# Layer one of a gated Flamingo stack: the second pair's rows prepared inside the first pair's scores, and maxima on four PSUM banks

## The chip, the cores and the metric

One core of one Trainium2 chip runs the whole program. TensorE (PE) multiplies matrices and transposes into PSUM, which has eight banks of 128 x 512 words. VectorE (DVE) and ScalarE (ACT) read PSUM; GpSimd (POOL) works on SBUF; SyncE (SP) issues transfers. The metric is the device time of one execution in microseconds (us).

## The reference

Four batches of 256 tokens x 256 features pass four layers, each with a gated attention and a gated feed-forward part. The change lies in the attention of layer one. Its setup fixes 16 heads of 16, keys and values from a 64-wide context:

```python
return {'q': jax.random.normal(k1, (B, S, H), dtype=jnp.float32), 'latent_kv': jax.random.normal(k2, (B, S, L), dtype=jnp.float32), 'Wq': ..., 'Wkv_expand': ..., 'Wout': ...}
```

What the kernel computes for each batch: rows of x are normalised (mean, variance); queries are their product with Wq; keys and values are the product of the context with Wkv; per head there is a causal softmax of the scores over 256 x 256; the weighted values of all heads go through Wout, and the result, times a gate, is added to x. Then comes the feed-forward part of layer one (ternary weights, 8-bit rows, a Hadamard transform), and layers two and three.

## The kernel before

**Tiling.** A token row lies on a partition; a batch is two tiles of 128 tokens (T = 2). Layer one's attention works on pairs of batches: turn i = 0 takes batches 0 and 1, turn i = 1 takes 2 and 3; inside a turn s = 0 or 1 is the batch. Every engine has its own instruction stream, in an order written out by hand, and waits on semaphores.

**Banks.** `plan(stage, i, ...)` gives each PSUM fill (a key such as `("max", 0, 3)`) a bank, in turn over a group's list of banks. A fill waits until its bank's previous fill has been read (`empty`); a reader waits until the fill is counted (`full`). In layer one, group A has the banks [4, 5], B the double banks [0, 2] (0-1 and 2-3), V the double bank 6-7.

**A turn's work, in PE's order.**
- `queries1`, `key_values1`: projections of a batch into B. ACT (`query_parts1`, `key_parts1`, L2149, L2156) writes their bf16 leading parts; DVE (`query_parts1`, `key_parts1`, L2817, L2827) writes the rests, the three-part split that lets bf16 products stand for float32. For s = 1 POOL finishes the parts (`parts1`, L949).
- `qsT`, `ksT` (`turn_column1`): the parts turned, four fills each for s = 0; ACT moves the queries out, DVE (`turned_keys`, L2805) the keys. For s = 1 they are the four double fills `cols`, between the maxima, moved by ACT.
- `max1` / `maximum1`: scores once more, only for their row maxima: 12 fills of a batch, which DVE reduces (L2851). The maxima are split and turned (`shift_rows1`, `shT`, L2864) and put by a small transfer into two rows of the queries' stack; PE waits for it (`shift_in`).
- `exp1` (L1405, L1407): the scores of two heads with the maximum taken off, 16 for a turn (g = 0 to 15); ACT exponentiates (L2182). `values1` (L1421) multiplies by the values, once for two `exp1`.
- `tokens1` turns the sums back to rows, DVE divides (`weighted1`, L2873, L2875), `turn_heads` turns them again, ACT moves them, `project` (L1446) multiplies by Wout, DVE adds into x (`add_projected`, L2882).
- `norm_next` (L2437 to L2471) normalises the next pair's rows; `turn_next` turns them, `queries1` follows.

**Other work on DVE.** `advance(largest, n)` does n pieces of the top-k search of layer two's adjacency, alternately two MAX8 (L2679) and two MATCH_REPLACE8 pairs (L2684); a 20th piece of a batch is L2687 and L2691. These pieces are spread by hand into places where DVE would wait.

**Between the two turns.** After the last `values1` and `project(0, 0)`, PE turns batch 2 and 3's rows, then interleaves batch 1's heads with the second pair's projections. `project(0, 1)` goes into bank 5 of A; `qsT` of turn 1 begins at bank 4, its second fill at bank 5.

Of the kernel before, what the change touches and what calls it, by code (L numbers as in the profile page):

```python
# [7 lines left out]
BF16 = mybir.dt.bfloat16  # L8
# [163 lines left out]
def flamingo_gated(nc, x, ctx_512, g_xattn, g_ffn, W_k0, b_k0, ln_gamma, ln_beta, gate_w, gate_b, expert_w, expert_b,  # L172
                   Wq1, Wkv1, Wout1, w_gate, w_up, w_down, Wq2, Wk2, gamma_raw, w12, w3, router_w, expert_bias,
                   sw1, sw2, sw3, W_router, W_sgate, Ws_gate_up, Ws_down, We_gate_up, We_down, consts, out):
    with ExitStack() as ctx:
# [316 lines left out]
        def plan(stage, i, **groups):  # L492
# [4 lines left out]
            for g, (firsts, wide, keys) in groups.items():  # L497
                f = pl.setdefault(stage, {}).setdefault(g, None) or Fills(sem(f"filled_{stage}{g}"))
# [29 lines left out]
        def max_order1():  # L528

            first = [("qsT", 0, k) for k in range(4)] + [("ksT", 0, k) for k in range(4)]  # L530
            for k in range(12):
                first += [("cols", 1, k // 3)] * (k % 3 == 0) + [("max", 0, k)]
            first += [("max", 1, 0), ("max", 1, 1), ("shT", 0)]
            return first + [("max", 1, k) for k in range(2, AHEAD1)]
# [5 lines left out]
        for i in range(TURNS):  # L540
            plan("l1x", i,
                 A=([4, 5], 1, [key for key in max_order1() if key[0] != "cols"]
                    + [("max", 1, k) for m in rest_at1 for k in rest_at1[m]] + [("shT", 1)]
                    + [("tok", 0, 0), ("tok", 0, 1), ("oT", 0), ("out", 0)]
                    + ([("xT", 0), ("xT", 1)] if i < TURNS - 1 else [("AT", 0), ("AT", 1)])
                    + [("tok", 1, 0), ("tok", 1, 1), ("oT", 1), ("out", 1)]),
                 B=([0, 2], 2, [("q", 0), ("kv", 0), ("q", 1), ("kv", 1)] + [("cols", 1, k) for k in range(4)]
                    + [("sc", s, k) for s in range(2) for k in range(NH1 // 2)]),
                 V=([6], 2, streams([("pv",)])))
        plan("prep1b", 0, A=([0, 1, 2, 3], 1, [("tern", w, k) for w in range(2) for k in range(2)]))  # L550
# [184 lines left out]
        def _(sp):  # L735
# [58 lines left out]
            f = pl["l1x"]["A"]  # L794
            for i in range(TURNS):
                for s in range(2):
                    sp.wait_ge(f.drained(i, ("shT", s)), f.read(i, ("shT", s)))
# [354 lines left out]
        def _(pe):  # L1152
# [207 lines left out]
            fa, fb = pl["l1x"]["A"], pl["l1x"]["B"]  # L1360
# [6 lines left out]
            def turn_column1(i, name, s, k):  # L1367
# [6 lines left out]
                else:  # L1374
                    turn(fa, i, (name, s, k), column_blocks(stack[s], pitch, 4 * k, 0), identb, BF16)

            def shift1(i, s):
                pe.wait_ge(shift_ready["l1x"].sem, shift_ready["l1x"].count(2 * i + s))
                turn(fa, i, ("shT", s), [(2 * NH1, t * P, sh1[s][:, t * 2 * NH1:(t + 1) * 2 * NH1]) for t in range(T)],
                     identb, BF16)  # L1380

            def max1(i, s, k):

                if k == 0:
                    for f, key in ([(fa, ("qsT", 0, 2)), (fa, ("qsT", 0, 3)), (fa, ("ksT", 0, 2)), (fa, ("ksT", 0, 3))] if s == 0
                                   else [(fb, ("cols", 1, 2)), (fb, ("cols", 1, 3))]):
                        pe.wait_ge(f.drained(i, key), f.read(i, key))
                pe.wait_ge(fa.drained(i, ("max", s, k)), fa.empty(i, ("max", s, k)))
                v = fa.slot(i, ("max", s, k))
# [6 lines left out]
                mm.then_inc(fa.filled, 1)  # L1396
# [13 lines left out]
            def values1(i, s, k):  # L1410

                fv = pl["l1x"]["V"]
                if k == 0:
                    pe.wait_ge(fv.drained(i, ("pv", s)), fv.empty(i, ("pv", s)))
                for m in (2 * k, 2 * k + 1):
# [23 lines left out]
            def project(i, s):  # L1439

                pe.wait_ge(fa.drained(i, ("oT", s)), fa.read(i, ("oT", s)))
                pe.wait_ge(fa.drained(i, ("out", s)), fa.empty(i, ("out", s)))
                v = fa.slot(i, ("out", s))
# [4 lines left out]
                mm.then_inc(fa.filled, 1)  # L1448
# [18 lines left out]
            def queries_turned1(i):  # L1467
                for k in range(4):
                    turn_column1(i, "qsT", 0, k)

            def scores1(i):

                for name, s, *k in max_order1():
                    if name == "max":
                        max1(i, s, *k)
                    elif name == "shT":
                        shift1(i, s)
                    elif name != "qsT":
                        turn_column1(i, name, s, *k)
                for g in range(NH1):  # L1480
# [12 lines left out]
                    if g == 12:  # L1493
                        tokens1(i, 0)
                    elif g == 14:
                        turn_heads(i, 0)
                values1(i, 1, 3)
                project(i, 0)
# [9 lines left out]
            turn_next("l1x", 0)  # L1508
            next_turned(fa, 0)
            queries1(1, 0)  # L1510
            tokens1(0, 1)
            key_values1(1, 0)
            turn_heads(0, 1)
            queries1(1, 1)
# [2083 lines left out]
```

## Time and profile before

| | |
|---|---|
| median of 3 runs | 772.85 us (770.63 to 774.46) |
| the profiled execution, its own time | 765.34 us |
| its span | 763.5 us |
| mean granted TensorE clock | 0.966 |
| PE busy | 670.3 us, 88% |
| DVE busy | 539.0 us, 71% |
| ACT busy | 351.9 us, 46% |
| POOL busy | 215.9 us, 28% |

Times in the rows count from the start of the span. Layer one's attention runs from 113 to 246 us. A timeline row gives start, length, engine, line, operation, tiles, count and, in brackets, how long its engine sat idle before it and what ended that. A PE row with a count has matmuls that overlap, so its length is that of the group.

### The profile page before, as it was taken

The numbers are of one execution on the slowest core, as the hardware profiler recorded it, in microseconds if no ns is written. First come the engines' busy times: TensorE is split into PE (matmuls) and PEld (weight loads), VectorE is DVE, ScalarE is ACT, GpSimd is POOL, SyncE is SP. The second block draws the span as 40 slices with busy tenths as digits, with TensorE's granted clock in tenths as the row PEclk, the third lists the DMA queues.
The fourth block names the chain that finished last, engine by engine and source line by source line (L and its number), as shares of the span: only waits on it lengthen the run. The fifth ranks groups of instructions, "written<-read, shape, count | busy, mean of one in ns | idle before, by whom it ended". The sixth has DMA issues, their size and how long they took to land. (4 is left out here: it accounts for less than half of the span.)

```text
span 763.5 us, 13913 instructions
## 1 busy us (share of the span) xinstructions
PE 670.3 (88%) x4446; PEld 457.7 (60%) x4446; DVE 539.0 (71%) x1622; ACT 351.9 (46%) x620; POOL 215.9 (28%) x308
## 2 busy tenths in 40 slices
PE   9999987897889877798889999976788999999997
PEld 4644565665666556567666787653243327777776
DVE  5787988879686597888887454546987967525545
ACT  2673445565454765432204524326478895212220
POOL 1002596001100023301333553643334220533330
PEclk9999999999899999999999999998789999999999
DMA  7996421040000050000034151012000034133314
GB/s 181 341 249 135 157 86 56 2 168 1 2 3 2 1 166 1 1 1 1 29 114 171 57 178 59 29 50 77 1 2 3 2 119 111 63 105 105 98 56 172
DMA packets 55565, 60.23 MB, mean 79 GB/s; under 512 B 13847, under 2 KB 48808, under 8 KB 55496
## 3 DMA queue, kind: packets, MB, share of 16 engines
q1 hardware_dynamic: 50408, 46.02, 21.2%
q0 software_dynamic: 4848, 13.28, 5.0%
q8 instruction: 38, 0.62, 0.4%
q14 instruction: 31, 0.25, 0.1%
q10 hardware_dynamic: 240, 0.05, 0.0%
HBM read 34.92 MB, written 24.20 MB: 77 GB/s over the span
## 5 line engine op out<-in xcount | busy, mean ns | idle before, releaser
L2016 ACT ACTIVATE arenas<-psum 128x512 f32<-128x512 f32 (+6 forms) x89 | 63.2, 732 | 58.5 <-PE psum L1175 50.6
L3295 DVE TENSOR_REDUCE arenas<-psum 128x2 f32<-128x512 f32 x96 | 61.8, 684 | 12.0 <-PE psum L1767 10.7
L1175 PE MATMUL psum<-conb,shared 128*128 128x128 bf16 (+2 forms) x512 | 41.1, 239 | 12.1 <-issue 8.1
L983 POOL TENSOR_SCALAR arenas<-arenas,small 128x1024 f32<-128x1024 f32 x8 | 9.0, 1124 | 150.9 <-DVE small L2986 150.9
L1175 PEld LDWEIGHTS psum<-conb,shared 128*128 128x128 bf16 (+2 forms) x512 | 36.0, 125 | 20.3 <-issue 17.8
L1000 POOL DMA_INDIRECT experts_l<-shared,small x30 | 29.7, 989 | 63.1 <-ACT shared L2318 52.7
L2016 ACT ACTIVATE late<-psum 128x512 f32<-128x512 f32 (+1 forms) x51 | 25.6, 502 | 42.6 <-PE psum L1175 42.5
L1175 PE MATMUL psum<-con,early 128*128 128x128 f32 (+1 forms) x188 | 32.2, 281 | 12.9 <-ACT late L2016 5.1
L2365 ACT ACTIVATE early<-psum 128x1024 f32<-128x1024 f32 x32 | 32.0, 1031 | 17.3 <-PE psum L1784 17.0
L1651 PE MATMUL psum<-arenas,early 128*128 128x256 f32 x160 | 36.7, 383 | 0.7 <-DVE arenas L3449 0.7
L2182 ACT ACTIVATE late<-psum 128x768 f32<-128x768 f32 x32 | 25.3, 811 | 24.7 <-PE psum L1407 24.5
L2851 DVE TENSOR_REDUCE arenas<-psum 128x2 f32<-128x512 f32 (+1 forms) x48 | 31.4, 686 | 6.9 <-PE psum L1394 6.5
L1651 PE MATMUL psum<-early,late 128*128 128x256 f32 x128 | 30.9, 388 | 5.9 <-DVE early L3188 5.8
L1175 PEld LDWEIGHTS psum<-con,early 128*128 128x128 f32 (+1 forms) x188 | 21.5, 143 | 23.6 <-ACT late L2016 8.1
L1148 POOL DMA_INDIRECT experts_l<-late,shared x23 | 22.0, 958 | 48.0 <-DVE shared L3469 41.9
L2365 ACT ACTIVATE late<-psum 128x1024 f32<-128x1024 f32 x32 | 31.4, 1062 | 5.0 <-PE psum L1784 5.0
L1175 PE MATMUL psum<-con,arenas 128*128 128x128 f32 x194 | 29.3, 279 | 4.9 <-DVE arenas L2471 2.6
L1164 PE MATMUL psum<-conb 128*128 128x512 bf16 x128 | 31.9, 401 | 1.8 <-POOLq L891 1.8
L2016 ACT ACTIVATE shared<-psum 128x256 f32<-128x256 f32 (+2 forms) x38 | 16.3, 429 | 36.8 <-PE psum L1175 31.6
L1651 PEld LDWEIGHTS psum<-arenas,early 128*128 128x128 f32 x160 | 29.8, 190 | 5.6 <-DVE arenas L3449 1.1
L3260 DVE TENSOR_TENSOR shared<-shared,psum 128x128 f32<-128x128 f32 x30 | 8.6, 287 | 33.7 <-PE psum L1720 19.6
L1720 PE MATMUL psum<-late,shared 128*128 x120 | 32.1, 390 | 0.2 <-issue 0.2
(455 smaller groups left out, 1770.4 us busy)
## 6 DMA issues: line engine op xcount, KB each, us to landing
sorted_l<-late SPq DMA_DIRECT2D x3, 1920.0 KB, 16.7
early<-sorted_l SPq DMA_DIRECT2D x6, 645.0 KB, 5.8
early<-in_L_ffn_sw SPq DMA_DIRECT2D x3, 1024.0 KB, 9.3
late<-sorted_l SPq DMA_DIRECT2D x23, 129.0 KB, 2.1
sorted_l<-late SPq DMA_DIRECT2D x1, 2944.0 KB, 23.2
early<-in_L_ffn_We_gate_up SPq DMA_DIRECT2D x2, 1408.0 KB
early<-in_L_ffn_expert_w SPq DMA_DIRECT2D x2, 1024.0 KB, 6.8
early<-in_L_ffn_w SPq DMA_DIRECT2D x1, 2048.0 KB, 8.4
```

Of the source, the lines that this page charges most:

```text
L983: pool.tensor_scalar(ha[s][:, rows], ha[s][:, rows], c2[s][:, t:t + 1], ROUND, ALU.mult, ALU.add)
L1000: pool.indirect_dma_start(expert_rows2[p], bass.IndirectOffsetOnAxis(dest2[p][:, i:i + 1], 0), out_r2[k], None).then_inc(outs_sent[k], 16)
L1148: pool.indirect_dma_start(expert_rows, bass.IndirectOffsetOnAxis(dest[i], 0), out_r[i % OUTS], None).then_inc(out_sent[i % OUTS], 16)
L1164: pe.matmul(v, onesb, onesb.unsqueeze(1).broadcast_to([P, BANK // P, P]), start=True, stop=True)
L1175: last = pe.transpose(v[0:parts, at:at + k], src, idn[0:k, 0:k])
L1651: mm = pe.matmul(v[0:rows, half * S:(half + 1) * S], w[:, c * width + at:c * width + at + rows], xT[s][:, c * S:(c + 1) * S], start=(c == ...
L1720: mm = pe.matmul(fu.slot(p, ("up", i))[:, 0:2 * H_R2], xT_r2[i % 2][:, c * P:(c + 1) * P], w12T[:, bass.ds(which[i] * (2 * H_R2) + c * E * ...
L2016: act.activation(dst, view(v), ACT.Copy, scale=scale).then_inc(f.drained(i, key), 1)
L2182: act.activation(q3d(pexp1[m % 4], 2, S + P), q3d(v, 2, BANK)[:, :, 0:S + P], ACT.Exp, scale=HD1 ** -0.5).then_inc(fb.drained(i, ("sc", s, ...
L2365: act.activation(pexp3[w // 4][m % 4], f.slot(0, ("sc", w, m)), ACT.Exp, scale=HD3 ** -0.5)\
L2851: dve.tensor_reduce(dst, q3d(v, heads, BANK // heads), X, ALU.max, negate=True) .then_inc(fa.drained(i, ("max", s, k)), 1)
L3295: dve.tensor_reduce(nm, q3d(f.slot(0, ("max", w, k)), 2, S), X, ALU.max, negate=True)\
```

## The change

1. Group A's early fills (`qsT`, `ksT`, the maxima of s = 0 and the first six of s = 1, `shT` of s = 0) become a group M over four banks [6, 7, 4, 5]; V still uses 6-7, and its first `values1` waits until the maxima there are read. `max1`'s waits for turned columns are made finer.
2. In turn 0, `turn_next("l1x", 0)` (the second pair's rows turned) stands at g = 14 of the scores; `next_turned` and `queries1(1, 0)` come ahead of the last `values1`. ACT moves the turned rows between the last two exponentials and takes `query_parts1(1, 0)` before `sums1(0, 1)` and `moved_heads(0, 0)`.
3. Batch 0's `turn_heads` moves behind the last `values1`. `project(0, 0)` comes after the second pair's `key_values1`, `queries1` and two of the four `qsT`; the other two `qsT` come behind `turn_heads(0, 1)`.
4. `project(0, 1)` and its `add_projected` move into turn 1, behind `shT` of batch 2, on a bank of M.
5. DVE: `weighted1(0, 0)` comes right after `norm_next`; `query_parts1(1, 0)` and the others are put between; 34 pieces of `advance` stay 34 but are dealt out anew (15 in turn 0 and 19 in turn 1, where there were 16 and 18).

```diff
             for g, (firsts, wide, keys) in groups.items():
-                f = pl.setdefault(stage, {}).setdefault(g, None) or Fills(sem(f"filled_{stage}{g}"))
+                f = pl.setdefault(stage, {}).setdefault(g, None)
+                f = f or Fills(None if (stage, g) == ("l1x", "V") else sem(f"filled_{stage}{g}"))
...
+        def out_at1(i, s):
+            return (1, ("out", 1, 0)) if (i, s) == (0, 1) else (i, ("out", s))
...
-            first += [("max", 1, 0), ("max", 1, 1), ("shT", 0)]
+            first += [("max", 1, 0), ("max", 1, 1), ("shT", 0)] + [("out", 1, 0)] * i
             return first + [("max", 1, k) for k in range(2, AHEAD1)]
...
             plan("l1x", i,
-                 A=([4, 5], 1, [key for key in max_order1() if key[0] != "cols"]
-                    + [("max", 1, k) for m in rest_at1 for k in rest_at1[m]] + [("shT", 1)]
-                    + [("tok", 0, 0), ("tok", 0, 1), ("oT", 0), ("out", 0)]
-                    + ([("xT", 0), ("xT", 1)] if i < TURNS - 1 else [("AT", 0), ("AT", 1)])
-                    + [("tok", 1, 0), ("tok", 1, 1), ("oT", 1), ("out", 1)]),
+                 M=([6, 7, 4, 5], 1, [key for key in max_order1(i) if key[0] != "cols"]),
+                 A=([4, 5], 1, [("max", 1, k) for m in rest_at1 for k in rest_at1[m]] + [("shT", 1)]
+                    + [("tok", 0, 0), ("tok", 0, 1)]
+                    + ([("xT", 0), ("xT", 1), ("oT", 0), ("tok", 1, 0), ("tok", 1, 1), ("out", 0), ("oT", 1)] if i == 0
+                       else [("oT", 0), ("out", 0), ("AT", 0), ("AT", 1),
+                             ("tok", 1, 0), ("tok", 1, 1), ("oT", 1), ("out", 1)])),
...
                 if k == 0:
                     pe.wait_ge(fv.drained(i, ("pv", s)), fv.empty(i, ("pv", s)))
+                    for n in range(AHEAD1 - 4, AHEAD1):
+                        pe.wait_ge(fm.drained(i, ("max", 1, n)), fm.read(i, ("max", 1, n)))
...
                     if g == 12:
                         tokens1(i, 0)
+                    elif g == 14 and i == 0:
+                        turn_next("l1x", 0)
                     elif g == 14:
                         turn_heads(i, 0)
+                if i == 0:
+                    next_turned(fa, 0)
+                    queries1(1, 0)
                 values1(i, 1, 3)
+                if i == 0:
+                    turn_heads(0, 0)
+                    key_values1(1, 0)
+                    tokens1(0, 1)
+                    queries1(1, 1)
+                    queries_turned1(1, range(2))
                 project(i, 0)
...
             scores1(0)
-            turn_next("l1x", 0)
-            next_turned(fa, 0)
-            queries1(1, 0)
-            tokens1(0, 1)
-            key_values1(1, 0)
             turn_heads(0, 1)
-            queries1(1, 1)
-            project(0, 1)
-            queries_turned1(1)
+            queries_turned1(1, range(2, 4))
             key_values1(1, 1)
             scores1(1)
...
+                    if g == 14 and i == 0:
+                        move_next(fa, 0)
+                if i == 0:
+                    query_parts1(1, 0)
+                    sums1(0, 1)
+                    moved_heads(0, 0)
+                else:
+                    moved_heads(i, 0)
+                    sums1(i, 1)
...
             def scores1(i):
-                advance(largest, (3, 4)[i])
+                advance(largest, 3)
                 turned_keys("l1x", i, 0, 4, K1 + 2, kT1)
...
                 if i == 0:
+                    advance(largest, 2)
                     for n in range(2, B):
                         experts_added0(n)
                     dve.drain()
                 norm_next("l1x", i)
-                advance(largest, (2, 5)[i])
-                weighted1(i, 0)
-                advance(largest, 4)
-                add_projected(i, 0)
-                if i == 1:
+                if i == 0:
+                    weighted1(0, 0)
+                    advance(largest, 5)
+                    query_parts1(1, 0)
+                    weighted1(0, 1)
+                    key_parts1(1, 0)
+                    query_parts1(1, 1)
+                    advance(largest, 2)
+                    add_projected(0, 0)
+                else:
+                    advance(largest, 5)
+                    weighted1(1, 0)
+                    advance(largest, 5)
+                    add_projected(i, 0)
                     symmetric(fa, i, 1)
-                advance(largest, (4, 2)[i])
-                weighted1(i, 1)
+                    advance(largest, 3)
+                    weighted1(i, 1)
+                    advance(largest, 3)
```

## Rows read from the trace of the kernel before

**Rows 1.** Busy time of each engine by stretch of layer one's attention; PEclk is the granted clock.
```profile
132.80:147.50 14.70, 11.46 (x156) 9.41 (x154) 12.07 (x23) 7.50 (x4) 2.32 (x3) 1.00 0.02 4
147.50:171.00 23.50, 21.63 (x302) 16.57 (x301) 18.83 (x58) 14.96 (x19) 0.00 (x0) 1.00 0.40 136
171.00:198.00 27.00, 21.91 (x134) 15.94 (x133) 20.08 (x53) 11.71 (x15) 2.32 (x3) 0.81 0.00 1
```

**Rows 2.** DVE's timeline, turn 0: keys moved, then the maxima.
```profile
128.59 1.29 DVE L2805 COPY arenas<-psum 98x1024 bf16<-98x1024 bf16 x2
132.23 0.69 DVE L2840 TENSOR_TENSOR late<-psum,shared 128x512 f32<-128x512 f32 x1 [0.20 <-issue]
...
133.50 2.10 DVE L2851 TENSOR_REDUCE arenas<-psum 128x4 f32<-128x512 f32 x3
...
141.33 1.99 DVE L2851 TENSOR_REDUCE arenas<-psum 128x2 f32<-128x512 f32 x3 [0.54 <-PE psum L1394]
...
144.97 0.27 DVE L2864 COPY arenas<-psum 32x256 bf16<-32x256 bf16 x1
```

**Rows 3.** PE's timeline: the first score of each turn.
```profile
147.80 0.28 PE L1405 MATMUL psum<-arenas 98*128 98x256 bf16 x1 [0.16 <-DMA arenas<-arenas]
...
213.45 0.28 PE L1405 MATMUL psum<-arenas 98*128 98x256 bf16 x1
```

**Rows 4.** PE's timeline between the turns.
```profile
166.78 0.66 PE L1175 MATMUL psum<-con,late 128*128 128x128 f32 x4
...
176.84 1.98 PE L1463 MATMUL psum<-early,arenas 64*128 64x512 f32 x4
...
180.98 1.93 PE L1446 MATMUL psum<-early,late 128*128 128x256 f32 x8
182.75 0.61 PE L1175 MATMUL psum<-conb,shared 128*96 128x128 bf16 x8
186.73 1.29 PE L1175 MATMUL psum<-conb,shared 128*96 128x128 bf16 x16 [3.37 <-issue]
```

**Rows 5.** DVE's timeline between the turns.
```profile
158.12 1.41 DVE L2437 BATCH_NORM_STATS2 small<-xs 128x6 f32<-128x256 f32 x4
...
163.53 0.75 DVE L2679 MAX8 small<-early 128x8 f32<-128x256 f32 x2
...
165.30 0.26 DVE L2873 RECIPROCAL arenas<-psum 128x16 f32<-128x16 f32 x1
...
166.64 0.74 DVE L2679 MAX8 small<-early 128x8 f32<-128x256 f32 x2
...
173.31 0.43 DVE L2687 TENSOR_SCALAR early<-early 128x512 f32<-128x512 f32 x1
...
174.90 0.76 DVE L2679 MAX8 small<-adj 128x8 f32<-128x256 f32 x2 [0.20 <-issue]
...
178.02 0.68 DVE L2791 TENSOR_TENSOR late<-psum,shared 128x512 f32<-128x512 f32 x1
...
182.18 0.69 DVE L2791 TENSOR_TENSOR late<-psum,shared 128x512 f32<-128x512 f32 x1 [0.24 <-issue]
...
185.88 0.75 DVE L2882 SCALAR_TENSOR_TENSOR xs<-psum,small,xs 128x512 f32<-128x512 f32 x1
```

**Rows 6.** DVE's timeline before turn 1's scores.
```profile
199.24 2.11 DVE L2851 TENSOR_REDUCE arenas<-psum 128x4 f32<-128x512 f32 x3
```

**Rows 7.** Busy time by stretches of 1 us, with the granted clock.
```profile
109.00:110.00 1.00, 0.00 (x0) 0.00 (x0) 0.92 (x3) 0.36 (x1) 1.00 (x2) 1.00 0.39 131
...
187.00:188.00 1.00, 1.00 (x15) 0.80 (x12) 1.00 (x5) 0.61 (x1) 0.71 (x2) 0.71 0.00 0
...
197.00:198.00 1.00, 1.00 (x15) 1.00 (x14) 0.72 (x2) 0.00 (x0) 0.00 (x0) 0.67 0.00 0
```

**Rows 8.** ACT's timeline between the turns.
```profile
169.91 1.01 ACT L2167 COPY arenas<-psum 128x1024 f32<-128x1024 f32 x1 [0.57 <-PE psum L1421]
...
176.08 1.51 ACT L2136 ACTIVATE shared<-psum 128x1024 bf16<-128x1024 f32 x2 [2.10 <-PE psum L1455]
```

## What I expect, and from what

> **What bounds the kernel now.** First the page's table of shares: PE is busy 88% of the span and DVE 71%, so a change in the order of work is worth what PE's idle time in its stretch is worth, and what TensorE loses to a low clock there. Then busy time by stretch [rows 1]: in the first turn's maxima (132.8 to 147.5) PE works 11.5 of 14.7 us and DVE 12.1; in the scores that follow PE works 21.6 of 23.5, PE sets the pace and nothing is to be had; between the turns (171 to 198) PE works 21.9 of 27.0 at a mean granted clock of 0.81. So two places hold slack: the maxima (twice) and the stretch between the turns. Then each engine's timeline. In the maxima DVE reduces three fills at a rhythm of 0.65 us and then idles 0.54 [rows 2], since two banks let PE be only two fills ahead and the turned `cols` come in between: a ping-pong. Between the turns PE stands still for 3.37 us until 186.73 [rows 4]. The trace names no releaser; it is the second `qsT`, on bank 5, which `add_projected(0, 1)` has to read first, and that DVE does at 185.88 to 186.63 [rows 5], behind everything else in its queue. Just after it the clock is at half (granted 0.50, which is 1.2 of 2.4 GHz), 187.3 to about 197.6 [rows 7].
>
> **Turn 0's maxima on four banks.** Keys: DVE starts moving them at 128.59 and today waits for the last two; with four banks all four are turned by then, so 4 x 0.65 = 2.6 us, to 131.2; then 0.1, and 1.27 for the values' part (132.23 to 133.50) gives the first maximum at 132.55 instead of 133.50, 0.95 less [rows 2]. The 12 maxima of s = 0 now take 133.50 to 143.32 = 9.8 us; without the waits 12 x 0.65 = 7.8, so 2.0 less. PE can hold that: three fills with their `cols` cost 0.89 + 3 x 0.34 = 1.9 us against DVE's 1.95 (my estimate from PE's rhythm; between the first and last maxima PE is busy 78% in rows 1), so they are nearly even, and if PE starts late it does not catch up. I take 2.5 of 2.95; the bounds are 1.5 (PE's late start costs one group) and 3.0. The transfer of the shift, 145.24 to 147.80 [rows 2, 3], stays. The first score then stands at 145.3 instead of 147.8. The prologue's queries on four banks gain nothing: the following `key_values1` waits for bank 2, which DVE frees at 124.5 either way.
>
> **Scores of turn 0.** 22 us to the last `values1`, PE's own work, unchanged. `turn_next` at g = 14 takes the place of `turn_heads` (166.78 [rows 4], so 164.1 now). It waits for the normalised rows. DVE, 2.5 earlier: two more pieces ahead (1.77, the pair from 163.53 to 165.30), two expert additions, then the normalising, 158.12 to 163.53 [rows 5]; shifted by 1.8 - 2.5 it ends at 162.85, 1.2 us in time. `weighted1(0, 0)` right behind (1.34, 165.30 to 166.64) frees bank 4 at 164.2, when PE wants it at 164.5: hidden, with little to spare.
>
> **Between the turns, walked through on PE** (durations: 8 transposes 0.9, a `queries1` or `project` 1.8, a `key_values1` 1.9, from the starts in rows 4; a pair of ACT's parts 1.5, the copy of the sums 1.0 [rows 8]). Rows turned to 165.0; last `exp1` and `values1` to 166.35; ACT's two moves are done by 166.1, so `next_turned` doesn't hold; `queries1(1, 0)` to 168.1; last `values1` 168.9; `turn_heads(0, 0)` 169.4; `key_values1(1, 0)` 171.3; `tokens1(0, 1)` wants ACT's copy (parts 168.2 to 169.7, copy to 170.7): ready; to 172.2; `queries1(1, 1)` to 174.0; two `qsT` (DVE's parts done at 172.0) to 174.9; `project(0, 0)` to 176.6; `turn_heads(0, 1)` to 177.1. All gaps of this stretch are filled up to here. The third `qsT` stands on bank 4, last filled by `("out", 0)`. So the wait is not removed; it changes its name to `add_projected(0, 0)`.
>
> When does DVE get there? It idles from 168.2 until ACT's parts at 169.7. Query parts 2.2 (178.02 to 182.18, less two pieces 1.8 and a gap) to 172.0; `weighted1(0, 1)` to 173.3; key parts 2.9 (182.18 to 185.88, less one piece 0.8), behind ACT, to 176.4; rest of the second queries 0.7 to 177.1; two pieces, one of them the long last one, 2.4 (173.31 to 175.66) to 179.5; `add_projected` 0.7 to 180.2 [rows 5]. PE stands 3.1 us, 177.1 to 180.2, almost what it stood before. Queued behind it: the two `qsT`, `key_values1(1, 1)`, `ksT` and all maxima. After it two `qsT` 0.9, `key_values1` 1.9, `ksT` 1.8: 184.9; DVE follows the keys, 183.6 to 186.2, and after 1.5 us for the values the maxima of turn 1 start at 187.7. Before it was 199.24 [rows 6]. From the first score of turn 0 this is 187.7 - 145.3 = 42.4 us against 199.24 - 147.80 = 51.4 [rows 3, 6]: 9.0 less, full clock assumed. It holds `project(0, 1)` (1.8) moved away, the idle bits ahead of 186.73 filled with work, and about 4.9 of work at half clock (from 186.73 to 198.12 PE does some 6.5 us of full-clock work).
>
> **Turn 1.** Four banks again: 2.0 less. `project(0, 1)`, 1.8 us on PE, falls into the wait for the shift's transfer, which is 2.5 us, so it costs nothing there; without that cover, 1.8. On DVE its addition (0.75) comes before the maxima 2 to 5 of s = 1, so the fills at g = 0 to 3 find banks 4 and 5 late, and PE loses some 0.7. The first score moves from 213.45 [rows 3] to 200.0 at full clock. At the end `weighted1(1, 1)` comes behind three pieces (2.6) instead of two (2.4 by the same rows): 0.3 with the rounding. The last three pieces fall under `turn_heads` and `project(1, 1)`. 15 + 19 pieces are 34, as before, so nothing goes to later stages.
>
> **Sum at full clock.** 2.5 + 9.0 + 2.0 - 0.7 - 0.3 = 12.5 us less.
>
> **The clock.** 3.37 us of idle PE before 186.73 were followed by half clock [rows 4, 7]. 1.85 us of idle, nearly all of 109 to 110.8, were not [rows 7]. The new wait of 3.1 us is nearer to the first. Right behind it stand 5.5 us of work that the maxima wait for. Bounds: nothing (no fall), and 4.7 (all of it and the first fills at half, as before). I take 2.5, about half. That is the forecast: 12.5 - 2.5 = 10.0 less. The Trainium skill, page "TensorE: Matmul & The Clock Gate", section "What's actually happening", says that the low clock is the default state and that activity releases it, and that there are just two levels. Rows 7 agree on the levels (a second of 0.71 or 0.67 is one that holds the step). By that rule the change is suspect in one more place, the next paragraph's second rival: whoever lets PE finish its maxima early buys it idle time.
>
> Against the profiled execution's 765.34 us this gives 755.3; the runs' median is 772.85, 7.5 above the profiled one, and the same 10.0 off it gives 762.9 us, 1.3% less. The measurement of this kernel tells some 0.5%, 3.9 us, from no change.
>
> **Rivals.**
> - *No fall of the clock in the new wait* (3.1 instead of 3.4 us of idle). For: 1.85 us did nothing. Against: the nearness of the two numbers. 12.5 less: 760.4. Chance 0.22.
> - *The clock falls already in turn 0.* With four banks PE waits 1.4 us for the shift's rows, works about 1.9 and then waits 1.9 for the transfer, where before the longest such wait was 0.5; then come the scores, PE's own work. Some 5 us at half cost 2.5, and with the full 4.7 later the gain is about 5.5: 767.3. For: the two idle pieces add up to 3.3. Against: there is work between them, and DVE-bound stretches ran at 1.00 in rows 1. Chance 0.15.
> - *The gain is given back.* The feed-forward part starts 10 us earlier and runs into something that was not waited for, or the deferred work costs as much as it saves (stalls at bank 4 for the rows' turning, at banks 4 and 5 in turn 1, 1.8 of uncovered projection). Then 0 to 4 less, 769 to 773. Against: the loads of the next weights are out by 171 and DVE's pieces are the same 34. Chance 0.12.
> - *Slower.* The same fall at the first score of turn 0 that lasts: PE's 21.6 us of scores [rows 1] at half clock take up to 21.6 more, a net 9 slower, 782. The point: low-clock work beyond 25 us in total (half of it is lost) eats 12.5. The longest low stretch here is 10 us [rows 7]. Chance 0.03.
> - The forecast itself: 0.48.
>
> **Numbers.** 762.9 us. The range of 8 in 10 leaves out the slow case and most of the given-back one on one side and a full-clock run with a lucky reading on the other: 758.0 (12.5 less, and 2.4 for the spread of the runs, which is 3.8 wide) to 769.0 (the second rival with the same allowance). Faster by over 0.5%: forecast, first and second rival, and a third of the given-back case: 0.88. Within: 0.09. Slower: 0.03.
>
> **What would show it.** First score of turn 0 at 145 to 146.3, DVE's maxima in one row of 0.65 without 0.5 gaps. An idle PE of about 3 us behind `turn_heads(0, 1)` that ends with `add_projected` (L2882's counterpart), with half clock behind it or not: this is the term I am least sure of. `turn_next` without a wait at g = 14. Maxima of turn 1 from 188 to 191. First score of turn 1 at 200 to 203, `project(0, 1)` just ahead of it with little idle time. I am wrong if DVE reaches `add_projected(0, 0)` much later, if the rows at g = 14 aren't ready, if clock falls multiply, or if the stages behind layer one's attention don't move up with it.

## The result, and the profile after

The changed kernel took 760.8 us (median of 4 runs, 758.5 to 761.6) against 773.1 (770.6 to 774.5): a ratio of 0.9863, with a 95% interval of 0.9823 to 0.9903. Forecast were 762.9 us in a range of 758.0 to 769.0.

The page of the changed kernel, its head and the busy time of the engines:

```profile
span 756.7 us, 13927 instructions
PE 666.9 (88%) x4446; PEld 457.0 (60%) x4446; DVE 538.1 (71%) x1622; ACT 351.2 (46%) x620; POOL 216.6 (29%) x308
```

The same work, 6.8 us less span than the trace of before. The two traces are one execution each, so the change is read from a stretch that both have: from the first key that DVE moves in turn 0 to the first reduction of the feed-forward part. Called the stage below, it took 118.25 us (128.59 [rows 2] to 246.84) and now takes 108.57 (130.24 to 238.81): 9.7 less. The rest of the difference is not the change's: the stage starts 1.65 later, behind a low-clock stretch at 111 to 119 that the trace of before did not have, and what follows it is 1.2 longer. The medians of the timed runs differ by 12.3 us, the ratio makes it 10.6, and 9.7 lies inside its interval (7.5 to 13.7 us).

The trace of before has a low clock of its own inside the stage, while the keys are turned, behind a wait of PE of 1.80 us. PE's row there, then DVE's, then 1 us of the clock:

```profile
129.39 3.59 PE L1175 MATMUL psum<-conb,shared 128*98 128x128 bf16 x32 [1.80 <-issue]
```

```profile
130.48 0.69 DVE L2805 COPY arenas<-psum 98x1024 bf16<-98x1024 bf16 x1 [0.60 <-PE psum L1175]
131.34 0.69 DVE L2805 COPY arenas<-psum 98x1024 bf16<-98x1024 bf16 x1 [0.16 <-PE psum L1175]
```

```profile
130.00:131.00 1.00, 1.00 (x13) 1.00 (x12) 0.52 (x1) 0.00 (x0) 0.00 (x0) 0.50 0.00 0
```

The last two keys come 0.86 us apart, the pace of turned keys at half clock in the changed kernel's turn 1 too (187.37, 188.22, 189.08). At full clock PE turns one in about 0.5 us (four in 1.99 us at 128.14 in the changed kernel), so the third would have been ready some 0.4 earlier and the fourth would not have held DVE. By this estimate about 0.5 us of what the keys give back below is the clock of that one execution and not the banks.

DVE's timeline of the changed kernel, turn 0, against [rows 2]:

```profile
130.24 2.49 DVE L2835 COPY arenas<-psum 98x1024 bf16<-98x1024 bf16 x4
...
134.21 7.46 DVE L2882 TENSOR_REDUCE arenas<-psum 128x4 f32<-128x512 f32 x12
...
143.32 0.27 DVE L2896 COPY arenas<-psum 32x256 bf16<-32x256 bf16 x1
```

All four keys in one row, and all 12 maxima without a gap: 7.5 us where 9.8 stood. The shift is copied 9.1 us after the first maximum begins, not 11.5. PE has become the engine that waits here, as its timeline shows (rows of the shift, then the first score, against [rows 3]):

```profile
142.35 0.27 PE L1188 MATMUL psum<-conb,arenas 128*32 128x128 bf16 x2 [1.00 <-DVE arenas L2890]
146.15 0.28 PE L1421 MATMUL psum<-arenas 98*128 98x256 bf16 x1 [1.81 <-DMA arenas<-arenas]
```

PE between the turns, against [rows 4]: the rows turned at g = 14 (no wait), then everything without a gap up to 178.4, then the wait.

```profile
164.86 1.07 PE L1188 MATMUL psum<-con,arenas 128*128 128x128 f32 x8
...
175.98 1.95 PE L1464 MATMUL psum<-early,late 128*128 128x256 f32 x8
177.77 0.60 PE L1188 MATMUL psum<-con,late 128*128 128x128 f32 x4
181.91 1.06 PE L1188 MATMUL psum<-conb,shared 128*96 128x128 bf16 x16 [3.54 <-issue]
182.90 3.41 PE L1481 MATMUL psum<-early,arenas 64*128 64x512 f32 x4
```

The trace names no releaser; DVE's timeline does, by time:

```profile
177.51 0.68 DVE L2855 TENSOR_TENSOR late<-psum,shared 128x512 f32<-128x512 f32 x1
178.11 0.42 DVE L2717 TENSOR_SCALAR early<-early 128x512 f32<-128x512 f32 x1
178.62 1.41 DVE L2721 SCALAR_TENSOR_TENSOR early<-adj,small,early 128x256 f32<-128x256 f32 x2
180.23 0.75 DVE L2709 MAX8 small<-adj 128x8 f32<-128x256 f32 x2 [0.20 <-issue]
181.06 0.75 DVE L2914 SCALAR_TENSOR_TENSOR xs<-psum,small,xs 128x512 f32<-128x512 f32 x1
...
192.09 7.47 DVE L2882 TENSOR_REDUCE arenas<-psum 128x4 f32<-128x512 f32 x12
```

L2914, `add_projected(0, 0)`, ends at 181.8 and PE goes on at 181.9. The clock behind it, by stretches of 1 us:

```profile
182.00:183.00 1.00, 1.00 (x17) 0.92 (x16) 0.93 (x4) 0.44 (x1) 0.00 (x0) 1.00 0.00 0
183.00:184.00 1.00, 1.00 (x2) 0.53 (x3) 0.93 (x6) 1.00 (x2) 0.00 (x0) 0.66 0.00 0
184.00:185.00 1.00, 1.00 (x2) 0.33 (x1) 0.38 (x1) 0.49 (x1) 0.00 (x0) 0.50 0.00 0
...
190.00:191.00 1.00, 1.00 (x19) 1.00 (x18) 0.80 (x2) 0.00 (x0) 0.00 (x0) 0.93 0.00 0
```

Turn 1 of the changed kernel on PE: the projection moved there, and the first score.

```profile
200.45 1.99 PE L1464 MATMUL psum<-early,late 128*128 128x256 f32 x8
...
204.70 0.28 PE L1421 MATMUL psum<-arenas 98*128 98x256 bf16 x1 [0.64 <-DMA arenas<-arenas]
```

Of the 1.8 us that PE waited for the same transfer in turn 0, 0.6 are left here: the projection stands inside it.

### The profile page after: what moved, and what is told of

It is laid out like the page before. It is cut to its first block and busy times, and to the rows that moved or that the text cites. A ratio compares the mean times of both kernels' runs of the same rounds, so it can differ in the third digit from the quotient of the medians.

```text
span 756.7 us, 13927 instructions
## 1 busy us (share of the span) xinstructions
PE 666.9 (88%) x4446; PEld 457.0 (60%) x4446; DVE 538.1 (71%) x1622; ACT 351.2 (46%) x620; POOL 216.6 (29%) x308
## 5 line engine op out<-in xcount | busy, mean ns | idle before, releaser
L3338 DVE TENSOR_REDUCE arenas<-psum 128x2 f32<-128x512 f32 x96 | 61.8, 684 | 12.1 <-PE psum L1791 10.7
L1188 PE MATMUL psum<-conb,shared 128*128 128x128 bf16 (+2 forms) x512 | 38.0, 230 | 9.6 <-issue 4.5
L1188 PEld LDWEIGHTS psum<-conb,shared 128*128 128x128 bf16 (+2 forms) x512 | 33.5, 118 | 17.3 <-issue 14.8
L1161 POOL DMA_INDIRECT experts_l<-late,shared x23 | 22.1, 962 | 48.6 <-DVE shared L3512 42.5
L1177 PE MATMUL psum<-conb 128*128 128x512 bf16 x128 | 31.6, 398 | 1.8 <-POOLq L904 1.8
```

The costliest lines, as they stand in the source:

```text
L1177: pe.matmul(v, onesb, onesb.unsqueeze(1).broadcast_to([P, BANK // P, P]), start=True, stop=True)
L1188: last = pe.transpose(v[0:parts, at:at + k], src, idn[0:k, 0:k])
L3338: dve.tensor_reduce(nm, q3d(f.slot(0, ("max", w, k)), 2, S), X, ALU.max, negate=True)\
```

## The experiments

Twelve runs of eleven kernels. All stage times are from one trace each; "between" is from the first score of turn 0 to the first maximum of turn 1. "Wait" is PE's wait ahead of the turned fills or, where named, elsewhere; "low clock" is where, between the turns or in turn 1's maxima, the granted clock is under 1, to the whole us. The ratio is to the kernel before on the same chip.

| kernel | keys to first score | between | turn 1 to its first score | to the end | stage | wait, low clock between the turns | ratio (95% interval) |
|---|---|---|---|---|---|---|---|
| before | 19.21 | 51.44 | 14.21 | 33.39 | 118.25 | 3.37, 187-198 | 1 |
| changed | 15.91 | 45.94 | 12.61 | 34.11 | 108.57 | 3.54, 183-191 | 0.9863 (0.9823-0.9903) |
| changed, again | 15.92 | 46.93 | 13.18 | 34.39 | 110.42 | 3.53, 180-191 | 0.9875 (0.9814-0.9935) |
| changed, third time | 15.90 | 46.10 | 12.81 | 34.30 | 109.11 | 3.54, 184-192 | 0.9889 (0.9854-0.9924) |
| four banks alone | 15.91 | 49.31 | 12.47 | 33.83 | 111.52 | 2.92, 188-195 | 0.9892 (0.9862-0.9923) |
| maxima on two banks | 18.34 | 46.32 | 16.37 | 34.09 | 115.12 | 3.54, 183-191 | 0.9963 (0.9925-1.0002) |
| heads weighed late | 15.91 | 51.25 | 13.05 | 34.32 | 114.53 | 4.02 and 3.54, 166-171 and 187-195 | one run |
| wait filled | 16.23 | 44.58 | 12.43 | 33.87 | 107.11 | 0.5, none | one run |
| add first | 15.90 | 42.81 | 14.01 | 34.25 | 106.97 | 0.6, none; 1.48, 187-191 later | 0.9807 (0.9737-0.9877) |
| keys and values first | 15.90 | 42.51 | 12.63 | 34.14 | 105.18 | 1.62, 182-187 | 0.9793 (0.9727-0.9859) |
| both | 15.90 | 42.81 | 13.75 | 34.36 | 106.82 | 0.28, none; 1.49, 191-195 later | 0.9801 (0.9741-0.9861) |
| rows late | 15.91 | 49.18 | 12.70 | 34.28 | 112.07 | 4.08, 184-195 | 0.9924 (0.9898-0.9949) |
| projection back | 15.92 | 48.77 | 11.89 | 35.68 | 112.26 | 3.58, 183-187 | one run |
| DVE's pieces dealt anew | 17.01 | 40.94 | 12.45 | 34.09 | 104.49 | 0.28, none | 0.9792 (0.9752-0.9832) |

**The changed kernel again**, unedited:

> The changed kernel once more, on the chip that also runs the three below. Times of the stage are taken in the trace from the first key that DVE moves in turn 0 to the first reduction of the feed-forward part: 118.25 us in the kernel before, 108.57 in the changed one. Theory (the walk along the engines' queues): 108.6 again, give or take 1.7 or 3.4 us where the clock falls once more or once less, and 1.2 to 1.7% less than before in time. Rival (the gain of the timed runs, 12.3 us, is more than the stage's 9.7 because of low-clock stretches elsewhere that have nothing to do with the change): the stage is as said, but the time moves by several us either way from one call to the next.

Stage 110.4, with the low clock 11 us long behind the same wait of 3.53 us, and ratio 0.9875: the gain repeats, and the stage moves by 1.9 us, with low clock at 180 to 191 as what differs. The third trace of the same kernel, at the end of the table, has 109.1 and 0.9889, where 108.6 or 110.3 and 0.980 to 0.988 had been expected. Against before, whose low clock between the turns was also 11 us long, the second trace is 7.8 shorter and not 9.7.

**Four banks alone.** The kernel before with group M, its waits, and nothing reordered:

```diff
-                 A=([4, 5], 1, [key for key in max_order1() if key[0] != "cols"]
-                    + [("max", 1, k) for m in rest_at1 for k in rest_at1[m]] + [("shT", 1)]
+                 M=([6, 7, 4, 5], 1, [key for key in max_order1() if key[0] != "cols"]),
+                 A=([4, 5], 1, [("max", 1, k) for m in rest_at1 for k in rest_at1[m]] + [("shT", 1)]
```

> The kernel before with the four banks alone: group M with its fills on banks 6, 7, 4, 5 and the waits that belong to it, all orders of PE, ACT and DVE as before. Theory: keys 0.9 less, maxima 2.4 less in each turn, the stall between the turns stays (the third turned fill stands on bank 4 behind add_projected(0, 1)) but two fills come ahead of it, 0.5 less: stage 118.25 - 6.2 = 112.0, time about 6 us less than before (ratio 0.992). Rival (the banks do it all, since the first two turned fills of turn 1 no longer wait for add_projected): the stage comes to 109 and the time to the changed kernel's.

Stage 111.5, forecast 112.0: 6.7 of the 9.7 us. Some 1.7 of these 6.7 is that the low clock between the turns lasted 7 us here and 11 before. The first theory holds; the wait between the turns is there, 2.9 us, two fills later than before. In time, 0.9892 cannot be told from the changed kernel's 0.9863 to 0.9889; the traces can, 111.5 against 108.6, with a low clock of nearly the same length behind the wait (against the changed kernel's other two traces it is 1.1 and 2.4).

**Maxima on two banks**, all else as in the changed kernel:

```diff
-                 M=([6, 7, 4, 5], 1, [key for key in max_order1(i) if key[0] != "cols"]),
+                 M=([6, 7, 4, 5] * 2 + [4, 5] * 10, 1, [key for key in max_order1(i) if key[0] != "cols"]),
```

> The changed kernel with only the maxima (and the shift and the projection among them) put back on banks 4 and 5; the turned queries and keys keep four. Theory: 2.4 more in turn 0 and 1.6 to 2.4 in turn 1, stage 112.6 to 113.4, time 4 to 5 us above the changed kernel. Rival (DVE was not held by the banks but by the order of the turned columns): stage 109 to 110, DVE's gaps between the reductions as long as with four banks.

Turn 0 gives back 2.4 us, as said, DVE's gaps of 0.5 are there again. Turn 1 gives back 3.8, more than said, so the stage is 115.1 where 112.6 to 113.4 was forecast, and the time 7.2 us above the changed kernel's on this chip where 4 to 5 was. DVE's timeline there shows why:

```profile
204.86 0.27 DVE L2896 COPY arenas<-psum 32x256 bf16<-32x256 bf16 x1
207.10 0.75 DVE L2914 SCALAR_TENSOR_TENSOR xs<-psum,small,xs 128x512 f32<-128x512 f32 x1 [1.97 <-PE psum L1464]
207.77 2.80 DVE L2882 TENSOR_REDUCE arenas<-psum 128x4 f32<-128x512 f32 x4
```

The projection waits for a bank, the maxima behind it for `add_projected`, and so the first score comes 4.8 us after the shift's copy and not 3.5. Moving the projection there is nearly free only because the banks are four: the two parts of the change lean on each other.

**Heads weighed late:**

```diff
-                    weighted1(0, 0)
                     advance(largest, 5)
+                    weighted1(0, 0)
```

> The changed kernel with one line moved: DVE does its five search pieces (4.4 us) before it weighs batch 0's heads and no longer after. Theory: the turned rows at g = 14 need banks 5 and 4, which that weighing frees, so PE stands some 4.0 us in the middle of the last scores and all that follows is 4.0 later: stage 112.6, and 1.7 to 3.4 more if the clock falls behind such a wait. Rival (the order of heads and search pieces is hidden, since DVE idles 1.4 us ahead of the queries' parts anyway): stage at most 1 us longer.

PE's timeline, the turned rows at g = 14:

```profile
167.22 1.94 PE L1188 MATMUL psum<-con,arenas 128*128 128x128 f32 x8 [4.02 <-DVE late L2907]
```

4.02 us for 4.0 forecast, and a low clock that begins within the wait, at 166, and lasts to 171. With both, "between" is 5.3 longer and the stage 114.5, in the 114.3 to 116.0 that the theory gave with a fall. The heads' weighing is where the reordering could have gone wrong; its margin is below half a microsecond (in the changed kernel it frees bank 5 at 164.5, and PE wants it at 164.9).

**Wait filled.** PE multiplies constants into an empty bank while it waits (`kept_busy` issues these products):

```diff
             turn_heads(0, 1)
+            kept_busy(fb, 1, ("kv", 1), 14)
             queries_turned1(1, range(2, 4))
```

> The changed kernel with 14 idle products of 512 columns on the still empty bank of the second pair's last keys and values, placed where PE waits for add_projected(0, 0). They compute nothing that is used. Their length is 3.0 us, as the wait. Theory (the wait costs twice: its own 3.5 us, and the half clock behind it): the third turned fill still starts when DVE has added, but the granted clock stays at 1.00, so the maxima of turn 1 start 2.9 us earlier after the first score (45.9 less 2.9, so 43.0) and the stage is 105.7. Rival (the low clock comes from elsewhere, or costs nothing as DVE sets the pace there): 45 to 46 and a stage of 108 to 109.

PE after the filled wait:

```profile
178.71 3.19 PE L1177 MATMUL psum<-conb 128*128 128x512 bf16 x14
182.41 1.06 PE L1188 MATMUL psum<-conb,shared 128*96 128x128 bf16 x16 [0.52 <-issue]
183.41 1.98 PE L1481 MATMUL psum<-early,arenas 64*128 64x512 f32 x4
185.32 2.88 PE L1188 MATMUL psum<-conb,shared 128*98 128x128 bf16 x48
```

The granted clock was 1.00 in each of 180 to 191. The same work takes 1.98 and 2.88 us where it took 3.41 and 4.72. From its start to the first maximum of turn 1 are 7.55 us (182.41 to 189.96), against 10.18 (181.91 to 192.09): 2.6 us for the low clock alone, with the wait kept. "Between" is only 1.4 shorter, since this execution had a low stretch at 146 to 150, at the first scores of turn 0, which is the second rival of the prediction, and its turned fills start 37.0 us after the first score and not 35.8. That is most of the reason why the stage came to 107.1 and not to the 105.7 of the theory.

**Three edits that take the wait away**, the first two together in the third:

```diff
                     query_parts1(1, 1)
-                    advance(largest, 2)
                     add_projected(0, 0)
+                    advance(largest, 2)
```

> The changed kernel with DVE's add_projected(0, 0) ahead of two search pieces (2.4 us) and not behind them. Theory: it runs at the end of project(0, 0), the stall of 3.5 us shrinks to some 0.6, the clock does not fall, and then DVE's five pieces hold the keys: maxima of turn 1 4.1 us earlier (41.8 after the first score), stage 104.5, time 0.5% under the changed kernel's. Rival (DVE is the bound there, the stall is only the other side of it): maxima at most 1 us earlier.

```diff
             turn_heads(0, 1)
+            key_values1(1, 1)
             queries_turned1(1, range(2, 4))
-            key_values1(1, 1)
             scores1(1)
```

> The changed kernel with key_values1(1, 1), 1.9 us of PE's work that has to wait for nothing, ahead of the two turned fills and so inside the stall. Theory: 1.7 us of the stall are left, no fall of the clock behind it, and DVE's pieces hold the keys: maxima of turn 1 3.7 us earlier (42.3), stage 104.9. Rival (what is left of the wait still drops the clock): 44 and 106.5.

> Both of the last two edits. Theory: PE no longer waits, DVE's queue alone sets the start of turn 1's maxima, so it adds nothing to either: 41.8 to 42.0 after the first score, stage 104.5. Rival (both stalls were PE's and add up): 39.9 and 102.5.

Maxima of turn 1 at 42.8, 42.5 and 42.8 us after the first score, where 41.8, 42.3 and 41.8 to 42.0 were forecast: 3.1 to 3.4 earlier than in the changed kernel, and together no more than alone. So beyond the wait it is DVE's queue that holds: in all three it goes from its search pieces to the keys without idling. One part of a theory failed: with keys and values first, the 1.62 us that is left of the wait still had a low clock behind it, 182 to 187; since DVE's pieces hold the keys, it cost next to nothing ahead of the maxima, 42.5 for 42.3. With DVE adding first, something new appears; PE in that kernel:

```profile
177.20 1.06 PE L1188 MATMUL psum<-conb,shared 128*96 128x128 bf16 x16 [0.59 <-issue]
178.19 1.98 PE L1481 MATMUL psum<-early,arenas 64*128 64x512 f32 x4
180.10 2.88 PE L1188 MATMUL psum<-conb,shared 128*98 128x128 bf16 x48
187.39 1.85 PE L1188 MATMUL psum<-conb,shared 128*96 128x128 bf16 x16 [1.48 <-issue]
```

PE is early, makes the first maxima, and then waits for DVE's values part to free a bank for the second `cols`; the clock falls at 187, and from the first maximum of turn 1 to the copy of the shift are then 10.7 us and not 9.1. The kernel with both edits does the same (1.49 us, low at 191 to 195). That eats half of the gain: stages of 107.0 and 106.8, where 104.5 was forecast for both; the kernel that uses the wait for keys and values has 105.2, forecast 104.9. The three ratios (0.979 to 0.981) cannot be told from one another, and this chip's runs of before were slower (785.3 us), so they are not set against ratios from another chip.

**Rows late**, the second pair's rows turned behind the last `values1`:

```diff
-                    elif g == 14 and i == 0:
-                        turn_next("l1x", 0)
...
                 values1(i, 1, 3)
                 if i == 0:
+                    turn_next("l1x", 0)
+                    next_turned(fa, 0)
+                    queries1(1, 0)
                     turn_heads(0, 0)
```

> The changed kernel with the second pair's rows turned after the last values1 and not at g = 14, and ACT's two moves after the last exponential. Theory: PE does the same work but then waits 0.5 to 0.7 us for ACT's moves, and the queries' parts reach DVE 1.5 us later; DVE's chain up to add_projected moves by that, PE's stall stays at 3.5, so all is 1.5 us later: 47.4 us from the first score to the maxima of turn 1, stage 110.1 (low clock as in the changed kernel). Rival (the place of the turning is what the change lives on, all of the order's 5 us): 51 and 113.5.

49.2 and 112.1, 1.8 and 2.0 above the forecast and 1.8 and 1.4 below the rival's, so the totals do not choose. The parts do: the turned fills start 37.8 us after the first score and not 35.8, which is 2.0 and not the 1.5 forecast (the queries' parts reach DVE 2.1 later, and PE's wait is 4.1); the other 1.2 comes behind the wait, with a low clock of 11 us and not 8. The place of the turning is worth some 2.0 us and what the clock adds.

**Projection back** between the turns (its addition behind the first one on DVE and its bank in group A are not shown):

```diff
             turn_heads(0, 1)
+            project(0, 1)
             queries_turned1(1, range(2, 4))
```

> The changed kernel with project(0, 1) back between the turns, behind turn_heads(0, 1), and its addition right behind the first one on DVE. Theory: 1.8 us of projection and 0.7 of addition come on the path between the turns, 2.6 in all, and 0.7 comes back in turn 1, where the project and its addition are gone from ahead of the maxima: 48.5 from the first score to the maxima of turn 1, stage 110.5. Rival (the projection fits into the stall as before, so its move gains nothing): 46 and 108.

48.8 between, forecast 48.5: 2.8 more than in the changed kernel, against 2.6 (its low clock between the turns was 4 us shorter, and it had one of 4 us at the first scores of turn 0, which about cancel). Turn 1 gets to its first score 0.7 sooner, and there PE waits 1.74 us for the transfer, where the projection had stood; a low clock at 206 to 211 follows, in PE's own scores, and the stretch to the end is 1.6 longer; so the stage is 112.3 where 110.5 was forecast. The projection's place gives 2.8 us between the turns, takes 0.7 of it back in turn 1, and may save a fall of the clock.

**DVE's pieces dealt anew**, with the two edits of before (34 pieces still):

```diff
                     weighted1(0, 0)
-                    advance(largest, 5)
+                    advance(largest, 6)
...
-                    advance(largest, 2)
                     add_projected(0, 0)
+                    advance(largest, 1)
...
-                advance(largest, 3)
+                advance(largest, (3, 1)[i])
                 turned_keys("l1x", i, 0, 4, K1 + 2, kT1)
...
                     elif name == "shT":
                         shift_turned1(i, s)
+                        advance(largest, i)
...
                     weighted1(1, 0)
-                    advance(largest, 5)
+                    advance(largest, 6)
```

> Made from what the runs showed: key_values1(1, 1) ahead of the two turned fills, add_projected(0, 0) right behind the second queries' rest, one of the two pieces there and two of the three ahead of the keys moved to where DVE idles (one more ahead of the queries' parts, one behind the shift in turn 1, one more behind weighted1(1, 0)); 34 pieces as before. Theory (after the stall is gone DVE's five pieces hold the keys): maxima of turn 1 at 39.5 us after the first score against 42.8 in the kernel with both edits, stage 103.5, time 0.4% under that and 0.7% under the changed kernel. Rival (PE's chain, and the wait of the cols for DVE's values part, hold it just as well): 41.5 to 42.5, stage 105 to 106.

> The changed kernel beside the one above, for a comparison of the two on one chip. Stage 108.6, or 110.3 with a longer low clock; ratio to before 0.980 to 0.988.

On one chip: 756.4 us against 763.0 for the changed kernel, 0.9792 (0.9752 to 0.9832) and 0.9889 (0.9854 to 0.9924) of before; the intervals do not touch. The stage is 104.5, 4.6 less, in an execution that had low-clock stretches at 125 to 133 and at 146 to 150. DVE's row ahead of turn 1's keys turns around:

```profile
182.69 2.48 DVE L2835 COPY arenas<-psum 98x1024 bf16<-98x1024 bf16 x4 [1.27 <-PE psum L1188]
185.44 0.69 DVE L2870 TENSOR_TENSOR late<-psum,shared 128x512 f32<-128x512 f32 x1 [0.26 <-ACT shared L2160]
```

Now DVE waits for PE there, 1.3 us. 40.9 came where 39.5 was forecast. The low clock in turn 0's scores accounts for 1.3 of the 1.4: PE turned batch 1's heads 32.9 us after the first score, and 31.6 in the kernel with both edits, and DVE was later by as much. That DVE would wait for PE was not in the theory: PE's chain, which the rival named, now sets the start of the keys. DVE's queue was some 1.2 us shorter than reckoned, and 1.1 of that is the pair L2721, 0.88 us here and 1.97 in the kernel with both edits; this hides the wait in the total, so the forecast is that near in part by luck.

## Why the prediction was right

Point by point, in its order, each against the traces:

- *Turn 0's four banks*, 2.5 in bounds of 1.5 to 3.0: measured 3.3 (15.91 us to the first score against 19.21), outside the bounds. 0.94 for the keys (0.95 said, about half of it perhaps the clock of before's execution, see above) and 2.36 for the maxima (2.0 said). I had held back 0.45 for a late PE; in ten of the twelve traces with four banks PE was not late, and the other two (16.23 and 17.01) had a low clock at 118 to 122 and at 125 to 132. The reductions also came at 0.62 us, not 0.65, once nothing stood between them.
- *The turned rows at g = 14 without a wait*: right. The heads' weighing as the near miss: right (0.4 us to spare), and shown by the run that moves it.
- *Between the turns at full clock*, 9.0 less: 5.5 measured with a low clock of 8 us. The filled wait put that clock at 2.6 us; so 8.1 at full clock. The wait changed its name and stayed: right in place and cause (shown by adding first: 0.6 us are left), 3.54 us where 3.1 was said. Counted from the first score, DVE's addition came 0.7 later than in the walk: 0.5 is one row, the last search piece's two L2721, which took 1.41 us together where before they took 0.88, and 0.2 is that ACT's parts came later. PE itself came 0.4 later.
- *The clock*, 2.5 of bounds 0 to 4.7: measured 2.6 by the filled wait, with a low clock of 8 us. Between the turns the fall came in all nine traces, that of before among them, that have a wait of 2.9 us or more there. The reason given was weaker than it looked: that 1.85 us of idle did nothing rested on one wait, and the trace of before has the 1.80 us ahead of 129.39 with a fall behind it. The Trainium skill, "TensorE: Matmul & The Clock Gate", "What's actually happening", has idleness lower the clock to one of two levels; the rows agree, 0.50 and 1.00 and nothing that lasts between. They also show a wait of 2.75 us with no fall behind it (changed kernel, to 126.23).
- *Turn 1*: 2.0 less for the banks, and 0.7 lost behind the projection. Measured 1.6 less to the first score, and 0.7 lost to the end, which also holds the 0.3 said for the tail. The 1.6 is 2.3 for the maxima less 0.7, since the first score comes 3.5 us after the copy of the shift and not 2.7. That is not the projection, for PE still waits 0.64 for the transfer behind it, and with four banks alone, where no projection stands there, it was 3.35; why the transfer lands later, no run shows. The projection hides in the transfer's wait: right, as that 0.64 shows; where it was put back between the turns, PE stood 1.74 us there instead.
- *Sum*: 10.0 said, 9.7 in the traces, 12.3 in the timed medians (10.6 by the ratio, 7.5 to 13.7). The mechanism holds, but that the sum came within 0.3 us is luck: turn 0 gave 0.8 more than its term, the stretch between the turns 1.0 less (5.5 for 9.0 less 2.5), turn 1 0.1 less, and with a low clock of 11 us, as in the second trace of the changed kernel, it is 7.8.
- *The rivals.* No fall of the clock: not here; with the wait filled it is 107.1. The fall at the first scores of turn 0, given 0.15, did not come in the changed kernel's three traces but in three of the nine others with four banks. The given-back case and the slower one did not come. That the banks do it all, the rival of the second run, is true by two thirds: 6.7 of 9.7 us, or 5.0 of 8.0 with some 1.7 us taken off both for the low clock that lasted 11 us before and 7 to 8 after.

What was least well put is the share of the parts: the order, with all its moves, is worth 3.0 us once the banks are there (1.1 to 3.0 by the three traces), because it kept a wait of 3.5 us and the low clock behind it. Taking that wait away gave about as much again: 3.4 us of the stage with keys and values first, and 4.6 with the pieces dealt anew as well.

Left open: how much of the scatter of whole runs (758 to 764 us in three sets of the changed kernel) is low-clock stretches elsewhere; each trace had some at 521 to 561 us, of other lengths each time. Nothing was tried there.

## What to carry to other kernels

When work is moved to fill an engine's idle time, ask at each bank or buffer that the next step needs who read it last, and where that read stands in its engine's queue: here the wait moved from one `add_projected` to another, and PE still stood 3.5 us there until one line went two pieces up. A wait of PE can cost twice, itself and the clock behind it (3.5 and 2.6 us here), and real work that waits for nothing is the best filling. More banks for the ping-pong of PE and DVE gave two thirds of this gain; then check that the filler work on the slower engine (here the search pieces) is not what holds the next stage.

## What the runs showed of the hardware

- The same two L2721 (SCALAR_TENSOR_TENSOR, 128x256, two operands in SBUF) took 0.88 us in the trace of before, 1.41 in the changed kernel and 1.97 in the one that adds first. What differs is POOL: idle in the first case, at work from 178.26 in the second and from 176.50 in the third, in both all the while. In all fourteen traces the pair took 0.88 where POOL was idle (before, four banks alone, DVE's pieces dealt anew), and 1.41 or 1.97 where it was at work. An earlier pair, near 109 us in the trace of before and with POOL at work in every trace, took 1.41 in all of them. POOL's two casts took 1.40 to 1.49 us beside the pair and 1.17 or 1.18 elsewhere. That POOL is the cause is argued from these cases, not tried by itself. A price read beside an idle POOL was too low by 0.5 to 1.1 us.
- The length of a wait alone did not tell whether the clock falls. It fell behind waits of 1.48 us (to 187.39, adding first), 1.49 (both edits), 1.62 (keys and values first) and 1.80 (before, to 129.39), and did not behind 2.75 (changed kernel, to 126.23) or 2.33 (first score of turn 1, four banks alone). At the 1.8 us ahead of turn 0's first score it fell in three of the twelve traces with four banks. What else decides it, the runs do not show.
- After the same wait of 3.5 us the clock stayed low for 8, 11 and 8 us in three executions of the same kernel, with PE busy from the wait's end on; the stage differed by up to 1.9 us between them.
